# A fused cross-attention and expert kernel: sums moved from TensorE to VectorE, products from VectorE to GpSimd, second buffers, and a new order for every engine

## The reference

```python
x = x + xattn(layernorm(x), ctx)     # Q = x Wq.T + bq; K, V from ctx; softmax(Q K.T / 4) V; Wo, bo
x = x + ffn(layernorm(x))            # E = 8 experts, F = 32 units each, top 2, LoRA rank 16
# ffn:
scores = softmax(x @ G);  w = one-hot(top-2 of scores) * value
gated  = silu(x @ gate_w) * (x @ up_w)
out    = (gated * w) @ down_w + ((x @ lora_A) * w) @ lora_B
```

## Time and profile before

| | us |
|---|---|
| median of 3 runs | 117.26 (117.11 to 117.43) |
| profiled execution | 117.28 |
| its span, first to last instruction | 115.5 |
| busy: PE, PEld | 108.6, 82.3 |
| busy: DVE, ACT, POOL | 91.4, 70.2, 49.4 |

### The profile page before, as it was taken

The page is one execution under the profiler, slowest core; times in us unless marked ns, Lnnn a source line. Parts: engine busy times, 40 slices in busy tenths (PEclk is TensorE's granted clock), DMA queues, the critical chain, the costliest instruction groups (busy, mean ns, idle before and its releaser), DMA issues.

```text
span 115.5 us, 2328 instructions
## 1 busy us (share of the span) xinstructions
PE 108.6 (94%) x892; PEld 82.3 (71%) x892; DVE 91.4 (79%) x192; ACT 70.2 (61%) x115; POOL 49.4 (43%) x79
## 2 busy tenths in 40 slices
PE   6999998999997999899999999999999999999780
PEld 6998677887885586586585766667778988586560
DVE  5436896999999997979999995899777998984410
ACT  0998528686878769895676796898427134313300
POOL 6929947499799920400052000222831674400000
PEclk9999999999999999999999999999999999999999
DMA  1999797474291002920000000000000000202022
GB/s 59 372 357 352 264 364 243 179 272 189 90 341 33 0 0 101 346 112 0 6 6 0 0 11 0 0 0 0 6 0 0 0 0 0 91 3 97 0 91 91
DMA packets 8453, 11.76 MB, mean 102 GB/s; under 512 B 697, under 2 KB 4986, under 8 KB 8442
## 3 DMA queue, kind: packets, MB, share of 16 engines
q1 hardware_dynamic: 7624, 10.83, 26.4%
q10 hardware_dynamic: 818, 0.79, 2.0%
HBM read 4.21 MB, written 1.05 MB: 46 GB/s over the span
## 4 chain that ended last, share of the span: by engine, by line
PE 61%; DVE 11%; ACT 7%; DMA 6%; SPq 5%; issue 4%; ACTq 2%; POOL 1%; POOLq 1%; DVEq 0%
PE unit L692 16%; PE unit L800 13%; PE unit L790 8%; PE unit L774 7%; DMA qstack<-q_lo 6%; PE unit L809 5%; PE unit L855 2%; PE unit L857 2%; PE unit L856 2%; DVE rowmax L616 2%; SPq L333 2%; ACT qstack L450 2%; PE unit L816 1%; ACT L450 1%; PE unit L842 1%
## 5 line engine op out<-in xcount | busy, mean ns | idle before, releaser
L616 DVE TENSOR_REDUCE rowmax<-unit 128x4 f32<-128x1024 f32 x32 | 37.6, 1221 | 3.5 <-PE unit L774 3.4
L502 ACT ACTIVATE probs<-unit 128x1024 f32<-128x1024 f32 x32 | 31.7, 1025 | 8.0 <-PE unit L790 7.3
L800 PE MATMUL unit<-probs,vaug 128*32 128x256 f32 x256 | 16.3, 384 | 0.0
L790 PE MATMUL unit<-qstack,kstack 64*128 64x256 f32 x128 | 13.1, 304 | 0.8 <-ACT probs L502 0.5
L774 PE MATMUL unit<-kstack,qstack 63*128 63x256 f32 x128 | 12.7, 302 | 0.8 <-DMA qstack<-q_lo 0.8
L790 PEld LDWEIGHTS unit<-qstack,kstack 64*128 64x128 f32 x128 | 9.2, 185 | 5.8 <-issue 2.9
L774 PEld LDWEIGHTS unit<-kstack,qstack 63*128 63x128 f32 x128 | 9.0, 185 | 4.2 <-issue 2.4
L435 POOL TENSOR_TENSOR x2T_lo<-x2T,x2T_hi 128x512 fp32r<-128x512 f32 x3 | 3.8, 1276 | 17.8 <-ACT x2T L517 17.8
L800 PEld LDWEIGHTS unit<-probs,vaug 128*32 128x32 f32 x256 | 7.1, 109 | 5.1 <-issue 0.2
L289 POOL TENSOR_TENSOR low<-low,weight_low 128x128 f32<-128x128 f32 x6 | 2.3, 402 | 14.5 <-DVE weight_hid L668 14.5
L692 PE MATMUL unit<-wf,x2T 128*128 128x136 f32 (+1 forms) x40 | 8.2, 344 | 0.0
(11 more groups left out here) (127 smaller groups left out, 222.6 us busy)
## 6 DMA issues: line engine op xcount, KB each, us to landing
kstack<-k_hi SPq DMA_DIRECT2D x8, 256.0 KB, 3.2
qstack<-q_hi SPq DMA_DIRECT2D x8, 256.0 KB, 3.0
xs<-x SPq DMA_DIRECT2D x4, 256.0 KB, 4.6
kstack<-k_lo SPq DMA_DIRECT2D x4, 256.0 KB, 2.4
qstack<-q_lo SPq DMA_DIRECT2D x4, 256.0 KB, 3.5
out<-xs SPq DMA_DIRECT2D x4, 256.0 KB, 2.1
wf<-wffn SPq DMA_DIRECT2D x1, 648.0 KB, 7.2
cT<-ctxT ACTq DMA_DIRECT2D x2, 256.0 KB, 4.9
```

The lines of the kernel that those rows point to most:

```text
L502: act.activation(probs[:, n % NPAIR], unit[BANK["attn", b, i] // 2][:], ACT.Exp, scale=SCALE)\
L616: dve.tensor_reduce(rowmax[:, b % 2, :, :, i].rearrange("p t j -> p j t"), unit[BANK["max", b, i] // 2][:], AX.X, ALU.max).then_inc(done[" ...
L790: ins = pe.matmul(pair[:, j, t], kstack[b][rows, i, t * P:(t + 1) * P], qstack[b][rows, i], start=True, stop=True)
L800: ins = pe.matmul(dst[QUAD * j:QUAD * (j + 1), i % 2], vaug[:, b % NVALUE, t, 4 * i + j], probs[:, n % NPAIR, j % 2, t], start=(t == 0), s ...
```

## The change

- `mean`, `mlow` and `bias`: VectorE adds the halves first (`ws`, `wsl`, `bw`), so each is one product on PE instead of two, two and three. `NWARM` goes from 13 to 11. `mlow` and `wlc` move from the start to the time of part 3's row maxima.
- `un` is split in three: `rd` (reciprocal, VectorE), `um` (product, now GpSimd) and `un` (turn back, VectorE).
- `chi` moves from GpSimd to ScalarE, `bp` from VectorE to ScalarE. ScalarE's `ex` applies the deviation itself and also gives the sum, in one instruction per tile; two VectorE operations go.
- `x2T_hi`, `x2T_lo`, `hidT` and `lT` have two buffers each; the second ones lie in tensors of the attention stage.
- Part 3's `down`, `res` and `out` are cut into two tiles.
- All five lists are new, found by a search. Counted in PE's list, runs of neighbouring `max` and `attn` stages fall from 26 to 22 (21 to 18 as far as `max:3.7`). `q:1` now stands ahead of `max:0.0`.

The diff, cut to its core (of the lists the new lines alone; the old ones stand in the kernel above):

```diff
-NWARM = 13
+NWARM = 11
...
+TILES = [[(0, 1)], [(0, 1)], [(0, 1)], [(0,), (1,)]]
...
 ORDERS = {
     "tensor": """
+        k:0@0 xT:0@1 v:0@2 q:0@1 mean@0 xT:1@3 bias@4 k:1@5 q:1@1 max:0.0@2 max:0.1@6 max:0.2@4 v:1@0 v:2@1
+        max:0.3@2 max:0.4@4 max:0.5@6 xT:2@0 k:2@1 max:0.6@2 max:0.7@4 q:2@0 max:1.0@6 max:1.1@4 xT:3@1 mrow:0@2
+        k:3@3 max:1.2@6 max:1.3@0 q:3@2 max:1.4@4 attn:0.0@6 max:1.5@0 attn:0.1@4 max:1.6@6 attn:0.2@2 max:1.7@0
+        attn:0.3@4 max:2.0@6 attn:0.4@2 max:2.1@0 mrow:1@4 u:0.0@5 attn:0.5@2 max:2.2@6 attn:0.6@0 u:0.1@5
+        max:2.3@2 attn:0.7@6 u:0.2@4 attn:1.0@0 attn:1.1@2 max:2.4@6 u:0.3@4 attn:1.2@0 attn:1.3@6 attn:1.4@2
+        u:1.0@5 max:2.5@0 max:2.6@2 o:0@4 attn:1.5@6 max:2.7@0 attn:1.6@2 u:1.1@5 max:3.0@6 max:3.1@0 mrow:2@4
+        x2T:0@2 mlow@3 v:3@5 attn:1.7@6 max:3.2@0 u:1.2@2 attn:2.0@4 max:3.3@6 attn:2.1@0 u:1.3@2 attn:2.2@4
+        max:3.4@6 low:0@3 attn:2.3@0 max:3.5@4 max:3.6@6 u:2.0@2 u:2.1@2 attn:2.4@0 max:3.7@4 attn:2.5@6
+        glu:0.0@3 attn:2.6@0 attn:2.7@4 mrow:3@6 o:1@7 glu:0.1@2 attn:3.0@0 attn:3.1@4 attn:3.2@6 u:2.2@3 u:2.3@3
+        attn:3.3@0 attn:3.4@4 x2T:1@2 u:3.0@3 u:3.1@3 attn:3.5@0 attn:3.6@4 attn:3.7@6 hT:0@2 low:1@3 o:2@0
+        u:3.2@1 u:3.3@1 x2T:2@0 lT:0@3 glu:1.1@4 low:2@2 lT:1@3 glu:1.0@5 o:3@0 glu:2.1@1 x2T:3@0 glu:2.0@2
+        low:3@0 hT:1@1 glu:3.1@3 lT:2@2 glu:3.0@4 hT:2@5 lT:3@0 down:0@1 hT:3@3 down:1@4 down:2@1 down:3.1@0
+        down:3.0@2
     """,
     "scalar": """
+        c:0 wq bo kfill:1 qfill:1 wkh wvh xTE:0 khi:0 chi:1 chi:2 n1:1 qhi:0 vE:0 xTE:1 khi:1 bp kw:1 qhi:1 qw:1
+        n1:2 vE:1 chi:3 vE:2 n1:3 xTE:2 wfh khi:2 kw:2 qhi:2 qw:2 xTE:3 mrE:0 khi:3 kw:3 qhi:3 e:0.0 qw:3 e:0.1-4
+        mrE:1 e:0.5-7 e:1.0-2 e:1.4 e:1.3 e:1.5-6 mrE:2 x2hi:0 x2w:0 vE:3 e:1.7 e:2.0-2 lowE:0 e:2.3-5 mrE:3 ex:0
+        th:0.0 e:2.6-7 th:0.1 e:3.0-3 x2hi:1 e:3.4 x2w:1 e:3.5-6 lowE:1 e:3.7 ex:1 hTE:0 x2hi:2 x2w:2 lTE:0
+        lowE:2 lTE:1 th:1.1 ex:2 th:1.0 th:2.1 x2w:3 th:2.0 lowE:3 hTE:1 ex:3 th:3.1 th:3.0 lTE:2 hTE:2 lTE:3
+        hTE:3
     """,
     "vector": """
+        warm edge kfill:2 st1:0 n1:0 st1:1 kfill:0 klo:0 ws:0 bw:0 qlo:0 st1:3 st1:2 wsl:0 wfc mx:0.0 mx:0.2
+        mx:0.1 mx:0.3-5 mx:0.7 mx:0.6 mx:1.0-7 mx:2.0-3 uT:0.0 rd:0.0 mx:2.4 uT:0.1 rd:0.1 un:0.0-1 mx:2.5-6 x2:0
+        mx:2.7 uT:1.0 mx:3.0-1 rd:1.0 wlc mx:3.2 un:1.0 mx:3.3 uT:1.1 mx:3.4 rd:1.1 mx:3.5-6 st2:0 mx:3.7 un:1.1
+        r1:0 uT:2.0 r2:0 rd:2.0 x2:1 h:0.0 r3:0 st2:1 h:0.1 uT:2.1 un:2.0 rd:2.1 un:2.1 uT:3.0 rd:3.0 un:3.0 r1:1
+        r2:1 x2:2 r3:1 uT:3.1 rd:3.1 st2:2 un:3.1 r1:2 r2:2 h:1.1 h:1.0 x2:3 r3:2 st2:3 h:2.1 h:2.0 r1:3 r2:3
+        r3:3 wl:3 h:3.1 h:3.0 wh:3 res:0 res:1 res:3.1 res:2 res:3.0
     """,
     "gpsimd": """
+        ident ones qfill:2 qfill:0 rs1:0 wkl rs1:1 clo:1 clo:2 earlier wvl rs1:3 rs1:2 klo:1 qlo:1 xo:0 xo:3
+        clo:3 xo:2 klo:2 qlo:2 xo:1 wfl klo:3 qlo:3 um:0.0 um:0.1 x2lo:0 um:1.0 um:1.1 rs2:0 um:2.0 wl:0 wh:0
+        um:2.1 rs2:1 um:3.0 x2lo:1 wl:1 um:3.1 x2lo:2 rs2:2 wh:1 wl:2 rs2:3 wh:2
     """,
     "sync": """
+        x:0 wk x:1 wv c:2 c:1 wf wo x:2 x:3 ks0:0 ks1:0 qs0:0 qs1:0 c:3 ks0:1 qs0:1 ks1:1 qs1:1 wd ks0:2 qs0:2
+        ms:0 qs1:2 ks1:2 ms:1 ks1:3 qs1:3 ks0:3 qs0:3 ms:2 ms:3 out:0 out:1 out:3.1 out:2 out:3.0
     """,
 }
...
-        x2T_hi, x2T_lo = sb("x2T_hi", [P, KT, S], F32R), sb("x2T_lo", [P, KT, S], F32R)
+        x2T_hi, x2T_lo = [sb("x2T_hi", [P, KT, S], F32R), wk_hi], [sb("x2T_lo", [P, KT, S], F32R), wk_lo]
...
+        wf_sum, low_sum, bo_terms = hid[:, 0].rearrange("p t f -> p (t f)"), low[:, 0, 0], hid[:, 1, 0]
+
+        hidT = [sb("hidT", [P, EF // P, S]), k_whole]
+        lT = [sb("lT", [P, S]), q_whole[:, 0]]
...
+                if name == "um":
+                    wait(pool, "rd", b, i)
+                    if b:
+                        wait(pool, "un", b - 1, i)
+                    pool.tensor_tensor(un[:, i].rearrange("p n h d -> p h n d"), uT[:, i, :, :, 0:HD],
+                                       rden[:, i].unsqueeze(3).to_broadcast([P, 2, BLK, HD]), ALU.mult).then_inc(done["um"], 1)
...
+                if name == "chi":
+                    act.wait_ge(c_in[b], 16)
+                    if b - 2 in KV_PARTS:
+                        wait(act, "k", b - 2)
+                        wait(act, "v", b - 2)
+                        wait(act, "clo", b - 2)
+                    act.copy(cT_hi[:, b % 2], cT[:, b]).then_inc(done["chi"], 1)
...
-                    act.activation(ex[:], below[:], ACT.Exp).then_inc(done["ex"], 1)
+                    wait(act, "rs2", b)
+                    for t in range(ST):
+                        ins = act.activation(ex[:, t], below[:, t], ACT.Exp, scale=rstd[:, 1, b, t:t + 1],
+                                             accum_out=esum[:, t:t + 1])
...
+                if name == "bw":
+                    dve.wait_ge(wo_in, 16)
+                    link(dve.tensor_scalar(bo_terms, wo[:, 0, 0:D], wo[:, 0, D:], None, ALU.mult))
+                    link(dve.scalar_tensor_tensor(out=bo_terms, in0=wo[:, 1, 0:D], scalar=wo[:, 1, D:], in1=bo_terms,
+                                                  op0=ALU.mult, op1=ALU.add))
+                    dve.wait_ge(bo_in, 16)
+                    dve.tensor_tensor(bo_terms[0:1], bo_terms[0:1], bo_row[:], ALU.add).then_inc(done["bw"], 1)
+                if name == "ws":
+                    wait_in(dve, wf_in)
+                    dve.tensor_tensor(wf_sum, wf[:, 0, 0:2 * EF], wf[:, 1, 0:2 * EF], ALU.add).then_inc(done["ws"], 1)
+                if name == "wsl":
+                    wait_in(dve, wf_in)
+                    dve.tensor_tensor(low_sum, wf[:, 0, 2 * EF:], wf[:, 1, 2 * EF:], ALU.add).then_inc(done["wsl"], 1)
...
+                if name == "rd":
+                    wait(dve, "uT", b, i)
+                    if b:
+                        wait(dve, "um", b - 1, i)
+                    dve.reciprocal(rden[:, i], uT[:, i, :, :, HD]).then_inc(done["rd"], 1)
                 if name == "un":
-                    wait(dve, "uT", b, i)
-                    link(dve.reciprocal(rden[:], uT[:, i, :, :, HD]))
-                    link(dve.tensor_tensor(un[:, i].rearrange("p n h d -> p h n d"), uT[:, i, :, :, 0:HD],
-                                           rden[:].unsqueeze(3).to_broadcast([P, 2, BLK, HD]), ALU.mult))
...
+                    wait(dve, "um", b, i)
                     if b >= 2:
                         wait(dve, "o", b - 2)
                     dve.transpose(attnT[:, b % 2, i], un[:, i].rearrange("p n h d -> p (n h d)")).then_inc(done["un"], 1)
...
-                    wait(dve, "down", b)
-                    dve.tensor_tensor(xs[:, b], work[BANK["down", b, 0]], xs[:, b], ALU.add).then_inc(done["res"], 1)
+                    wait(dve, "down", b, i)
+                    part = slice(TILES[b][i][0], TILES[b][i][-1] + 1)
+                    dve.tensor_tensor(xs[:, b, part], work[BANK["down", b, i]][:, part], xs[:, b, part], ALU.add)\
+                        .then_inc(done["res"], 1)
...
-                    wait_in(pe, wo_in)
-                    pe.wait_ge(bo_in, 16)
-                    for k in range(KT):
-                        pe.matmul(dst[:, 0], wo[:, k, D:].to_broadcast([P, P]), wo[:, k, 0:D], start=(k == 0), stop=False)
-                    pe.matmul(dst[:, 0], warm[0:1], bo_row[:], start=False, stop=True).then_inc(done["bias"], 1)
+                    wait(pe, "bw")
+                    pe.matmul(dst[:, 0], warm[:], bo_terms, start=True, stop=True).then_inc(done["bias"], 1)
                 if name == "mean":
                     wait(pe, "ones")
-                    pe.wait_ge(wf_in, 16)
-                    for k in range(KT):
-                        ins = pe.matmul(dst.rearrange("p o f -> p (o f)"), mean[:], wf[:, k, 0:2 * EF],
-                                        start=(k == 0), stop=(k == KT - 1))
-                    ins.then_inc(done["mean"], 1)
+                    wait(pe, "ws")
+                    pe.matmul(dst.rearrange("p o f -> p (o f)"), mean[:], wf_sum, start=True, stop=True).then_inc(done["mean"], 1)
                 if name == "mlow":
                     wait(pe, "ones")
-                    pe.wait_ge(wf_in, 16)
-                    for k in range(KT):
-                        ins = pe.matmul(dst[:, 0, 0:LOW], mean[:], wf[:, k, 2 * EF:], start=(k == 0), stop=(k == KT - 1))
-                    ins.then_inc(done["mlow"], 1)
+                    wait(pe, "wsl")
+                    pe.matmul(dst[:, 0, 0:LOW], mean[:], low_sum, start=True, stop=True).then_inc(done["mlow"], 1)
```

More of the change, by code:

```diff
@@ L52 @@
[L52 to L56, removed]
@@ L241, in wait_evacuated @@
             if name == "down":
-                wait(engine, "res", b)
+                wait(engine, "res", b, i)
             if name == "bias":
@@ L431, in _ @@
                     wait(pool, "x2w", b)
[L432 to L435, removed]
+                    if b >= 2:
```

(36 more changed lines are left out.)

56 lines of the change are left out of this document (14 added, 42 removed).

## The result

The changed kernel takes 116.42 us in the median of 19 runs, the kernel before 117.30 in 19: a ratio of 0.9922 (95% interval 0.9907 to 0.9937). That is a gain of 0.9 us; 2.0 were forecast. The direction held, the range held the time, and the size was off by more than half. The changed kernel's 19 executions go from 115.37 to 117.64, and the ratio is taken without the four slowest of them, from 117.16 on.

A forecast was written before the change was run, and what follows sets the result against it. PE's work and what comes before and after it were taken as the bound: 18.9 + 89.3 + 2.3 + 3.0 = 113.5 span, + 1.78 = 115.3 us, 1.7% below the median. The range for 8 in 10 was 112.6 to 117.6.

The forecast's parts named there:

- The start: Up to the first row maximum: it comes at 18.9 us, 0.5 later than before, bounds 17.6 and 20.3.
- PE's work from there: From first row maximum to PE's last product: 89.3 us, after `q:1` moves ahead and four `max`/`attn` runs go.
- Its waits there: PE's idle time from the first row maximum on: 2.3 us, bounds 0.8 and 5.
- Tail: After PE's last product: half-sized `res` (0.69 to about 0.42) and store (some 0.1) cut 3.37 to 3.0 us.
- Outside the span: Profiled time beyond the span: 1.78 us, added as before.
- The late start: Rival at the start: first row maximum at its bound of 20.3, time 116.7 us; chance 0.13.
- The middle: First row maximum to PE's last product: 89.3 us of PE's work plus 2.3 us of waits.
- GpSimd's product: `um`, moved from VectorE to GpSimd: 0.68 us each, eight of them, with room in GpSimd's list.
- the first rival: At the eight `un`, VectorE waits 0.88 each for GpSimd to save 0.47; up to 118.6 us; chance 0.12.
- the third rival: Behind `mx:3.7`, five `um` each block a VectorE operation for 0.68; a third on the path gives 116.4 us; chance 0.08.

The follow-up runs named there:

- the kernel as it is: The changed kernel run again unaltered, on the chip of the next three runs: 116.39 us, ratio 0.9911 to the kernel before.
- `wkl` later: Changed kernel with GpSimd doing `wkl` after `rs1:1` instead of before it: 115.12 us, ratio 0.9809 to the kernel before.
- both repairs: Changed kernel with `bias` as three products on PE without `bw`, and `wkl` behind `rs1:1`: 114.37 us, ratio 0.9753.
- the last three versions: `bias` on PE, GpSimd's second query fill behind `clo:2`: 113.93 us; that with `earlier` between `wkl` and `clo:1`: 113.96; the first with `mean` on PE, no `ws`: 113.91.
- the two runs of the tail and the product: Changed kernel with part 3's `down`, `res`, `out` in one piece: 116.75 us; changed kernel with the product of `un` back on VectorE: 116.43 us.
- the version with `earlier` between: `bias` on PE, GpSimd's second query fill behind `clo:2`, `earlier` between `wkl` and `clo:1`: median 113.96 us; profiled executions 113.0, 112.83 and 113.06.

## Why the prediction was off: the start, term by term

**The step that failed is "The start"**, in two terms of it: `n1:0` at 0.73, and `ws` and `bw` at 1.95 with an upper bound of 2.4. Neither was priced beside GpSimd. They measured 1.68 and 4.18. That `n1:0` would meet `wkl`, and `bw` would meet `clo` and `wvl`, stands nowhere in the forecast. In its sum `bw` ended at 14.4, just ahead of PE's `bias` at 13.1 + 0.86 + 0.6 = 14.56, so that no wait was counted there, and the first scores hung on the query stack's DMA. In the run `bw` ended at 17.37, `bias` started at 17.43, and the first scores followed PE's own `k:1` and `q:1`.

The mechanism was at hand, as the 1.00 us beside `x2lo`. The line behind the 0.17 that the forecast set against it, from the trace of before:

```profile
L661 DVE SCALAR_TENSOR_TENSOR ex<-rank,ex 128x16 f32<-128x16 f32 x4 | 1.5, 380 | 0.1
```

By the Trainium skill (SBUF — State Buffer, "Who interferes with whom") an operation of VectorE that needs the pair of ports shared with GpSimd is blocked for the whole of the instruction that was issued first; the Trainium skill counts there a two-input operation beside a GpSimd read, and a `tensor_scalar` that can use both ports. The traces agree with it at `n1:0` (0.73 or 1.68), L639 (0.48 or 1.37) and L642 (0.41 or 1.37).

The prediction placed this only behind `mx:3.7`, where it gave it a chance of 0.08. It didn't follow GpSimd's list along the new times of VectorE's. With `rs1:0` 1.3 us later (6.79 for the 5.51 of the earlier trace rows), `n1:0` meets `wkl`, which before began at 8.57, 1.26 us after `n1:0` had ended. The delay itself was forecast well (6.9). It is one half of the meeting; the other is that `wkl` begins 0.55 us sooner than before (8.02).

The sum, forecast against measured:

| Term | Forecast | Measured | Difference |
|---|---|---|---|
| First scores of `max` | 18.9 (17.6 to 20.3) | 21.22 | +2.3 |
| PE's work from there | 89.3 | 88.9 | -0.4 |
| Its waits there | 2.3 | 1.3 | -1.0 |
| Tail | 3.0 | 3.15 | +0.15 |
| Outside the span | 1.78 | 1.81 | 0 |

Together +1.1: 115.3 + 1.1 = 116.4. The start alone would have given 117.6, the upper end of the range; that the time came out nearer is owed to terms that were off the other way. The late start was among the rivals, and its grounds (the two fills and VectorE's longer list) named the right place, but nothing in them was a meeting of the two engines, and its bound of 20.3 was too low.

**The middle** was right and a little pessimistic. From first scores to PE's last product the traces have 111.45 - 21.19 = 90.3 us in the kernel as it is, 110.17 - 19.89 = 90.3 with `wkl` later, 109.66 - 19.39 = 90.3 with both repairs: a constant, wherever the start ends (only the product on VectorE makes it 90.65). So what the start loses goes to the end whole, and what is repaired there comes back whole. Fewer runs of `max` and `attn` and one `q:1` less gave together what the sum said; its terms weren't tested one by one. (The end of `max:3.7` before is 64.37 by the earlier trace rows, not 64.30, which changes nothing.)

**GpSimd's product**: 0.62 for 0.68, with room. VectorE doesn't stand for it: 1.9 us in all, against the 0.88 each of the first rival. The lock behind `mx:3.7`, the third rival, doesn't show either: PE isn't idle from 50 to 90, and the operation that took 1.00 in the earlier trace rows is short in all four parts:

```profile
L710 DVE SCALAR_TENSOR_TENSOR ex<-rank,ex 128x16 f32<-128x16 f32 x4 | 0.7, 181 | 0.1
```

The last `mx` begins at 67.95, 2.3 beyond the middle of its forecast, as the start is.

**The tail**: 0.27 + 0.1 forecast for the halves, 0.32 to 0.36 measured.

**What stays open** is the spread of the last three versions, 112.8 to 114.9, where the kernel as it is, `bias` on PE, `wkl` later, both repairs and the two runs of the tail and the product agree within 0.3 each. For one of the three a cause is seen in one profile (the tie of `ws` and `clo`); taking the tie away left the median where it was. For the version with `earlier` between, three of the four executions at 113.9 or more had a mean granted clock of 0.985, against 0.997 to 1.00 in the four at 113.1 or less; the fourth had 1.00. None of the four at 113.9 or more has a profile, so that is a correlation and no more. In the changed kernel four of the five executions above 117 had 0.985 too; but one at 116.41 and, with the product on VectorE, one at 116.37 had it and lost nothing.

The version with both repairs is the fastest of the steady ones (114.28 to 114.41): 114.37 us, 2.5% below the kernel before; the three versions behind it are at 113.9 in the median. A start without the new sums on VectorE for `bias` is better than one with them.

## What to carry to other kernels

Before an operation is priced from its row, look at what GpSimd does in that row and what it will do beside the operation at its new time: a delay that is right to the tenth can still move two operations onto each other. Work moved from PE to VectorE ahead of the first long stage is free only if it ends before PE comes by; here two products of `bias`, 1.1 us of PE's time, cost 1.7 us of waiting. Where two engines begin within 0.1 us of each other, take more than one execution before you trust a time. A short operation put between them made `ws` short in all three profiles here, but didn't better the median.

## What the runs showed of the hardware

- A GpSimd fill, which reads nothing, held up a VectorE `tensor_scalar` of 128x256 with one tensor input: 3.25 us for two instructions over a fill and a remainder, 0.73 with GpSimd idle.
- A VectorE operation on one row of 256 values took 1.37 us behind a GpSimd operation of 1.46, and 0.41 when it began 0.12 ahead of it. `ws` took 0.68 when it began 0.01 ahead of `clo`, 1.81 when it began 0.01 behind. Who begins first goes first, and a small operation waits as long as a large one.
- GpSimd pays as well: `clo:1` and `clo:2` together took 2.49 with `mean` on PE, and 2.95 to 3.08 with `ws` beside them.
- In the repeat of the kernel as it is, the granted clock was 0.50, the lower level of 1.2 GHz, in the slices from 11 to 14 us, after PE had been idle for 1.9 us behind `k:0`; an idle time of 1.70 there, with the bias on PE, left it at 1.00. So did one of 1.95 with `rs1:0` ahead of the second fill, so the length of the idle time alone doesn't tell. The lower clock cost nothing there: `v:0` took 2.90 instead of 1.89, but `bias` began at 17.43 in both executions, since it waits for L642; the wait fell from 1.67 to 0.68. Busy time by stretch from 11 to 12 us, first of that execution, then of the one with the idle time of 1.95:

```profile
11.00:12.00 1.00, 1.00 (x4) 0.74 (x4) 1.00 (x1) 1.00 (x3) 0.92 (x3) 0.50 1.10 355
```

```profile
11.00:12.00 1.00, 1.00 (x6) 0.88 (x5) 1.00 (x1) 1.00 (x4) 0.86 (x2) 1.00 1.06 339
```
